# Seven blocks of z kept side by side in float32, with one cast and one subtraction a pair

## The reference

```python
h   = maximum(layernorm(x), 0)                  # x is (8192, 256)
mask = (adj > 0);  deg = sum(mask, axis=1)      # adj is (8192, 8192) int32
agg = mask @ h / maximum(deg, 1)
self_f = h @ W_self + b_self
nb_f   = agg @ W_nb + b_nb
out = x + relu(concat(self_f, nb_f) @ W_comb + b_comb)
```

## Time and profile before

| | us |
|---|---|
| median of 3 runs | 914.53 (914.16 to 917.45) |
| the profiled execution | 915.82 |
| its span, first to last instruction | 914.0 |
| TensorE matmul busy | 896.9 (98%) |
| VectorE busy | 799.1 (87%) |
| ScalarE busy | 377.5 (41%) |
| GpSimd busy | 91.0 (10%) |

### The profile page before, as it was taken

One profiled execution on the slowest core, in us unless ns is written; L12 is line 12 of the kernel. 1 busy time (PEld: TensorE's weight loads), 2 busy tenths in 40 slices (PEclk: granted clock), 3 DMA queues, 4 the chain that ended last, 5 costly groups with the idle time before them and its releaser, 6 DMA issues. The chain is left out here.

```text
span 914.0 us, 19105 instructions
## 1 busy us (share of the span) xinstructions
PE 896.9 (98%) x7720; PEld 760.1 (83%) x7720; DVE 799.1 (87%) x1512; ACT 377.5 (41%) x358; POOL 91.0 (10%) x132
## 2 busy tenths in 40 slices
PE   7999899899999999999999999999999999999997
PEld 5555478788888888888888888888888888888886
DVE  5999898898998988898889888888899998888884
ACT  3999854233333333332333333333333333333320
POOL 2888820000000000000000000000000000000000
PEclk9999999999999999999999999999999999999999
DMA  6467769999999999999999999999999999999950
GB/s 213 162 220 274 265 233 391 400 370 388 376 384 377 378 380 377 373 370 368 367 380 377 389 392 370 381 365 364 358 374 372 380 386 379 369 376 376 398 211 22
DMA packets 61367, 312.80 MB, mean 342 GB/s; under 512 B 6880, under 2 KB 8032, under 8 KB 28512
## 3 DMA queue, kind: packets, MB, share of 16 engines
q1 hardware_dynamic: 60736, 311.06, 87.7%
q10 hardware_dynamic: 544, 0.52, 0.2%
HBM read 294.78 MB, written 16.78 MB: 341 GB/s over the span
## 5 line engine op out<-in xcount | busy, mean ns | idle before, releaser
L625 PE MATMUL banks<-t,operands 128*128 128x257 f16 x7168 | 786.5, 272 | 2.6 <-DVE work L757 2.6
L625 PEld LDWEIGHTS banks<-t,operands 128*128 128x128 fp8e4 x7168 | 698.3, 97 | 90.7 <-issue 2.8
L468 ACT ACTIVATE mask<-stage,few 128x2048 fp8e4<-128x2048 int32 x128 | 252.7, 1999 | 415.5 <-DVE turned L720 318.9
L705 DVE TENSOR_SCALAR mask<-stage 128x2048 uint8<-128x2048 int32 x128 | 154.5, 1226 | 5.8 <-DMA stage<-in_adj_dram 5.8
L565 PE MATMUL banks<-t,xh 128*128 128x512 f16 x384 | 89.3, 383 | 4.2 <-DVE t L698 3.1
L757 DVE TENSOR_TENSOR work<-banks,work 128x512 f32<-128x512 f32 x32 | 22.1, 692 | 74.8 <-ACT work L518 74.8
L734 DVE TENSOR_TENSOR operands<-turned,operands 128x1024 uint32<-128x1024 uint32 x64 | 78.4, 1225 | 8.8 <-DVE turned L720 0.5
L714 DVE STREAM_TRANSPOSE operands<-mask 128x512 uint32<-128x512 uint32 x128 | 83.1, 687 | 0.2 <-DVE t L693 0.2
L720 DVE STREAM_TRANSPOSE turned<-mask 128x512 uint32<-128x512 uint32 x128 | 80.8, 669 | 0.0
L736 DVE TENSOR_TENSOR operands<-turned,operands 128x1024 uint32<-128x1024 uint32 x64 | 78.2, 1222 | 0.0
L565 PEld LDWEIGHTS banks<-t,xh 128*128 128x128 f16 x384 | 37.7, 98 | 44.0 <-issue 4.6
(11 more groups left out here) (62 smaller groups left out, 391.4 us busy)
## 6 DMA issues: line engine op xcount, KB each, us to landing
stage<-in_adj_dram SPq DMA_DIRECT2D x256, 1024.0 KB, 8.5
out_dram<-operands SPq DMA_DIRECT2D x32, 256.0 KB, 2.8
xh<-in_x_dram SPq DMA_DIRECT2D x32, 256.0 KB, 9.5
own<-out_dram SPq DMA_DIRECT2D x32, 256.0 KB, 10.5
out_dram<-xh SPq DMA_DIRECT2D x32, 256.0 KB, 6.0
t<-in_x_dram SPq DMA_DIRECT2D x30, 256.0 KB, 4.4
turned<-in_x_dram SPq DMA_DIRECT2D x2, 256.0 KB, 5.4
t<-in_L_gnn_W_nb_dram ACTq DMA_DIRECT2D x1, 256.0 KB, 4.0
```

The lines of the kernel that those rows point to most:

```text
L468: act.activation(mask[:, b, :].bitcast(FP8), stage[:, b, :], ACT.Sigmoid, bias=steep, scale=STEEP, saturate=False).then_inc(formed_s, 1)
L625: mm = pe.matmul(banks[:, n, 0:width], bytes_of[:, c, :, s], t16[:, KQ * h + SUB * c + s, SLOT[n], 0:width], start=(h == 0 and c == 0 and ...
L705: dve.tensor_scalar(mask[:, b, :], stage[:, b, :], 0.0, float(MINUS_ONE_BYTE), ALU.is_gt, ALU.mult).then_inc(formed_v, 1)
```

## The change

- `kept` holds all seven blocks of z and the own part of a pair (1408 columns). Two places lie in the second slot of `operands`, the third in `work`. The eviction writes the own part first and four z blocks behind it; GpSimd writes its three blocks behind these. One cast of 896 columns and one subtraction of 896 columns replace two each. The next eviction into a place waits for the whole subtraction.
- The columns of `w12` lie in another order, and the projection's right side is a pattern of two runs of 256 columns.
- Pairs 3, 7, 11, ... have both tiles normalized by ScalarE; GpSimd leaves these out.
- The start: 22 transposes of the identity instead of 16; the bias loads go ahead of the first weight loads on SP's queue; GpSimd instead of VectorE spreads the biases into `b_wide`; the negated weights are made in two halves; the product of the biases comes ahead of the first projection, projections 0 and 1 follow each other, and the turns come after them by `TURNS_AFTER`; VectorE makes the low halves of w and of h(1) ahead of the next statistics.
- The first adjacency blocks are loaded, formed and transposed in other iterations. Of step 2, `make_third` comes ahead of the loop over r.

```diff
-WARM = 16
+WARM = 22
-DIRECT = 4
-W_SUM, W_F1, W_OWN, W_F2, W_MINUS = 0, P, 2 * P, 4 * P, 5 * P
+W_OWN, W_SUM, W_F1, W_F2, W_MINUS = 0, 2 * P, 3 * P, 4 * P, 5 * P
-FORM_STEPS_S = {20: A12, 22: A21}
-FORM_STEPS_V = {23: A22, 25: A11}
-TURN_STEPS_V = {24: A22, 26: A11}
+FORM_STEPS_S = {20: A12, 23: A21}
+FORM_STEPS_V = {19: A22, 21: A11}
+TURN_STEPS_V = {20: A22, 22: A11}
-NEXT_STEPS_V = {27: A22, 28: A11}
+NEXT_STEPS_V = {25: A22, 28: A11}
-LOAD_STEPS = {12: A12, 14: A21, 16: A22, 18: A11}
-NEXT_LOADS = {21: (1, A12), 23: (1, A21), 24: (1, A22), 26: (1, A11), 28: (2, A22), 29: (2, A11)}
+LOAD_STEPS = {10: A22, 11: A11, 13: A12, 15: A21}
+NEXT_LOADS = {20: (1, A22), 22: (1, A11), 23: (1, A12), 25: (1, A21), 27: (2, A22), 29: (2, A11)}
+TURNS_AFTER = {1: (2, 3), 2: (4,), 3: (5,), 4: (6, 7)}
 def norms_s(j):
-    return (0,)
+    return (0, 1) if j >= 3 and j % 4 == 3 else (0,)
 def norms_g(j):
-    return () if j < 3 else (1,)
+    return () if j < 3 or j % 4 == 3 else (1,)
...
+        KEPT = 2 * D + 7 * P
+        slot_1 = operands[:, 1, :, :].rearrange("p o w -> p (o w)").bitcast(F32)
+        kept = [slot_1[:, 0:KEPT], slot_1[:, KEPT:2 * KEPT], work[:, :, :, :].rearrange("p n c m -> p (n c m)")[:, 0:KEPT]]
+        def kept_z(j):
+            return kept[j % RING][:, 2 * D:KEPT].rearrange("p (c m) -> p c m", c=7)
...
             def store_own(j):
                 sp.wait_ge(evicted, j + 1)
-                sp.dma_start(out[j, :, :].rearrange("p (t d) -> p t d", t=2), kept_blocks(j)[:, 2:6, :].rearrange("p (t f) m -> p t (f m)", t=2)
-                             ).then_inc(own_stored[j % RING], DONE)
+                sp.dma_start(out[j, :, :], kept[j % RING][:, 0:2 * D]).then_inc(own_stored[j % RING], DONE)
...
             load_x(0)
             load_x(1)
+            sp.dma_start(b_cols, b_cols_in[:, :]).then_inc(b_loaded, DONE)
+            sp.dma_start(bc_row, b_comb.rearrange("(a n) -> a n", a=1).partition_broadcast(P)).then_inc(b_loaded, DONE)
             sp.dma_start(ws_t, w_self_t.rearrange("(h p) n -> p h n", p=P)).then_inc(w_loaded[0], DONE)
...
+            pool.wait_ge(b_loaded, 2 * DONE)
+            for m in range(2 * HALVES):
+                pool.tensor_copy(b_wide[:, m, :], b_cols[:, m:m + 1].to_broadcast([P, P])).then_inc(wide_ready, 1)
             root_of(0)
+            pool.wait_ge(sum_high, 1)
+            pool.tensor_scalar(w12[:, 0, :, W_MINUS:W_WIDE], w12[:, 0, :, W_SUM:W_F1], -1.0, None, ALU.mult
+                               ).then_inc(sum_negated, 1)
             pool.wait_ge(sum_ready, 1)
-            pool.tensor_scalar(w12[:, :, :, W_MINUS:W_WIDE], w12[:, :, :, W_SUM:W_F1], -1.0, None, ALU.mult
+            pool.tensor_scalar(w12[:, 1, :, W_MINUS:W_WIDE], w12[:, 1, :, W_SUM:W_F1], -1.0, None, ALU.mult
                                ).then_inc(sum_negated, 1)
-            for b in range(1, 3):
-                root_of(b)
+            root_of(1)
...
+                if j == 0:
+                    root_of(2)
...
-                    act.wait_ge(t_low, 2 * (j - RING) + 1)
-                act.activation(kept[:, j % RING, :, :], pair_ps[j % RING][:, :, :], ACT.Copy, scale=Z_SCALE).then_inc(evicted, 1)
+                    act.wait_ge(t_low, j - RING + 1)
+                act.activation(kept[j % RING][:, 0:4 * D].rearrange("p (a t w) -> p t a w", a=2, t=2),
+                               pair_ps[j % RING][:, :, :].rearrange("p t (a w) -> p t a w", a=2), ACT.Copy, scale=Z_SCALE
+                               ).then_inc(evicted, 1)
 
             def high_of_t(j):
-                act.wait_ge(evicted, j + 1)
-                act.activation(direct_in_t(j, 0), direct(j), ACT.Copy).then_inc(t_high, 1)
                 act.wait_ge(combined, j + 1)
-                act.activation(t16[:, j, DIRECT:7, 0:P], combos[:, j % RING, 0:3, :], ACT.Copy).then_inc(t_high, 1)
+                act.activation(t16[:, j, :, 0:P], kept_z(j), ACT.Copy).then_inc(t_high, 1)
...
-            project(0)
             pe.wait_ge(wide_ready, 2 * HALVES)
...
-            turn(2)
-            for j in range(1, PAIRS):
-                if j + 2 < PAIRS:
-                    turn(j + 2)
+            for j in range(PAIRS):
                 project(j)
+                for n in TURNS_AFTER.get(j, (j + 3,) if j >= 5 else ()):
+                    if n < PAIRS:
+                        turn(n)
...
             def low_of_t(j):
-                dve.wait_ge(t_high, 2 * j + 1)
-                dve.tensor_tensor(direct_in_t(j, P), direct(j), direct_in_t(j, 0), ALU.subtract).then_inc(t_low, 1)
-                dve.wait_ge(t_high, 2 * j + 2)
-                dve.tensor_tensor(t16[:, j, DIRECT:7, P:D], combos[:, j % RING, 0:3, :], t16[:, j, DIRECT:7, 0:P],
-                                  ALU.subtract).then_inc(t_low, 1)
+                dve.wait_ge(t_high, j + 1)
+                dve.tensor_tensor(t16[:, j, :, P:D], kept_z(j), t16[:, j, :, 0:P], ALU.subtract).then_inc(t_low, 1)
...
             low_of_h(0)
+            w_low(0)
+            low_of_h(1)
             for p in range(2, 4):
                 stats_of(p)
-            w_low(0)
+            dve.wait_ge(c_product, 1)
+            dve.tensor_tensor(c_row[:, :], pair_ps[2][:, 0, 0:D], bc_row, ALU.add).then_inc(c_ready, 1)
             shifts(1)
...
             make_second(2)
+            make_third(2)
             for r in range(PAIRS):
                 i = 2 * r + 3
                 merge_a(r)
                 outer_sums(r)
-                if r == 0:
-                    make_third(2)
```

More of the change, by code:

```diff
@@ L149, in x_pair @@
             return flat_t[:, p * PLACE:p * PLACE + 4 * D].bitcast(F32)
-        kept = operands[:, 1, :, :].rearrange("p o w -> p (o w)").bitcast(F32)[:, 0:RING * 4 * D].rearrange(
-            "p (n t d) -> p n t d", n=RING, t=2)
-        def kept_blocks(j):
-            return kept[:, j % RING, :, :].rearrange("p t (c m) -> p (t c) m", c=4)
-        def direct(j):
-            return kept[:, j % RING, :, :].rearrange("p t (h b m) -> p (t h) b m", h=2, b=2)[:, 0:4:3, :, :]
-        def direct_in_t(j, first):
-            return t16[:, j, 0:DIRECT, first:first + P].rearrange("p (h b) m -> p h b m", h=2)
+        KEPT = 2 * D + 7 * P
[3 more added lines that the diff above has]
+            return kept[j % RING][:, 2 * D:KEPT].rearrange("p (c m) -> p c m", c=7)
         w_sum = own[:, 0, 0, :].rearrange("p (h m) -> p h m", h=HALVES)
         w_second = own[:, 0, 1, :].rearrange("p (h m) -> p h m", h=HALVES)
-        combos = work
         flat_work = work[:, :, :, :].rearrange("p n c m -> p (n c m)")
@@ L493, in _ @@
             w_high_half(0)
+            high_of_h(1)
             for t in norms_s(2):
@@ L497, in _ @@
             for j in range(PAIRS + 2):
-                if j + 1 < PAIRS:
+                if 1 <= j < PAIRS - 1:
                     high_of_h(j + 1)
@@ L556, in project @@
                     pe.wait_ge(sum_ready, 1)
-                    pe.wait_ge(sum_negated, 1)
+                    pe.wait_ge(sum_negated, 2)
                 if j >= RING:
@@ L564, in project @@
                     for at, (half, i, w) in enumerate(steps):
-                        mm = pe.matmul(pair_ps[j % RING][:, t, :], h_t[:, j % RING, i, t, half, :],
-                                       w12[:, w, half, t * W_OWN:t * W_OWN + 2 * D],
+                        mm = pe.matmul(pair_ps[j % RING][:, t, :].rearrange("p (a n) -> p a n", a=2), h_t[:, j % RING, i, t, half, :],
+                                       w12[:, w, half, :].rearrange("p (a n) -> p a n", a=3)[:, 0:2 + t:1 + t, :],
                                        start=(at == 0), stop=(at == len(steps) - 1))
@@ L615, in product @@
                 if i == 0 and n == M4:
-                    pe.wait_ge(t_low, 2 * KQ)
+                    pe.wait_ge(t_low, KQ)
                     pe.wait_ge(ones_set, 2 * len(ONES_OF))
@@ L852, in _ @@
                 norm(2, t)
-            dve.wait_ge(b_loaded, 2 * DONE)
-            for m in range(2 * HALVES):
-                dve.tensor_copy(b_wide[:, m, :], b_cols[:, m:m + 1].to_broadcast([P, P])).then_inc(wide_ready, 1)
             for p in range(4, 6):
@@ L890, in _ @@
             dve.wait_ge(combined, PAIRS)
-            dve.wait_ge(t_low, 2 * PAIRS)
+            dve.wait_ge(t_low, PAIRS)
             make_second(1)
```

20 lines of the change are left out of this document (6 added, 14 removed).

## The result

The changed kernel takes 919.15 us (median of 16 runs) beside 914.21 us for the kernel before (16 runs): a ratio of 1.0049 with an interval from 1.0036 to 1.0062. It is slower, by about 4.5 us, where 910.0 us was predicted: clear of no change, and on the line of 0.5% itself.

A forecast was written before the change was run, and what follows sets the result against it. TensorE was taken to bound the steady preamble, with the adjacency products untouched. Start 2.0 + late gaps 2.2 + hand-over 0.3 = 4.5 us gained: 910.0 us against the median of 914.53 us, range 906.5 to 914.5 us.

The forecast's parts named there:

- I estimate the biases landed at 6.3 us: Start, GpSimd's copies ahead of the first root: root at 7.5 us, 0.5 us late, bounds 0 and 1.2.
- Nothing: Steady pairs of the preamble: merged cast and subtraction, moved normalizations and new outer wait were to change the time by nothing.
- The cover I named: Steady pair: ScalarE needs about 2.8 of 3.03 us, and TensorE's turn comes about 2.6 us after VectorE's low half.
- the slow rival: Preamble bound by a ring of ScalarE and VectorE, 0.35 us more a pair over 28 pairs: 919.8 us, chance 0.09.
- The late gaps: TensorE's gaps late in the preamble: 2.5 us expected instead of 4.7, so 2.2 us gained, bounds 0.5 and 4.7.
- The end gap: Last preamble gap, 1.3 us ahead of 114.83 us: it goes, since VectorE's two late blocks are asked for four steps sooner.
- Turn 26: Late preamble, the four transposes of pair 26: expected some 2.2 us late, before about 1.2.
- The hand-over: From preamble to adjacency stage, with its stall of 2.6 us at 171.9 us: 0.3 us gained, bounds -0.5 and 2.6.
- The clock rival: Clock falls in the new 2.4 us gap ahead of projection 2, costing 1.7 us: 911.7 us, chance 0.18.
- The ring of ScalarE and VectorE: Preamble: their chain of halves, statistics, subtraction, eviction and cast exceeds 6.06 us for two pairs: 919.8 us, chance 0.09.
- the old gap: Start: TensorE stood from 12.75 to 15.84 us ahead of the first projection, waiting for VectorE's second low half of w.
- the cast's price: Steady pair on ScalarE: one cast of 896 columns near 0.93 us, 0.12 us cheaper than the two before.

The follow-up runs named there:

- e1: The changed kernel with GpSimd's first root ahead of the four bias copies: 915.57 us, ratio 1.0012 to the kernel before.
- e5: The changed kernel with the first root ahead of the bias copies and VectorE's subtraction in two: 913.86 us, ratio 0.9991 to the kernel before.
- e6: e1 with VectorE's shifts behind the subtraction, which stays whole: 913.39 us, ratio 0.9986 to the kernel before.
- e3: The changed kernel with normalizations divided as before, one tile of every pair on ScalarE, the other on GpSimd: 918.49 us, ratio 1.0031 to the kernel before.
- e12: e6 with VectorE's low half of h(2) and third shift ahead of the statistics of pairs 6 and 7, and GpSimd's later roots one iteration later: 912.66 us.
- e4: The changed kernel with the third phase of step 2 back inside the loop, after the first merge: 919.31 us, ratio 1.0036 to the kernel before.
- e11: e6 with the normalizations divided between ScalarE and GpSimd as before: 913.23 us, ratio 0.9987 to the kernel before.
- e8: e1 with the load of block A22 of step 2 in iteration 28, as before, instead of 27: 917.62 us, ratio 1.0028 to the kernel before.
- e7: e1 with each own store issued as two transfers of 1 KB a partition: 918.0 us, ratio 1.0039 to the kernel before.
- e10: e6 with forming, turning and loading of the first adjacency blocks in the iterations of the kernel before: 918.98 us, ratio 1.0056 to the kernel before.
- e2: The changed kernel with VectorE's subtraction of 896 columns split into 512 and 384: 916.77 us, ratio 1.0018 to the kernel before.

## Why the prediction was wrong, step by step

**The step that failed first: "I estimate the biases landed at 6.3 us".** They landed at 8.9 us, and the first root stood behind them. The prediction named this as what would make it wrong, and bounded it at 1.2 us; it was 2.86 us on the root. Taking it back gave 3.8 us at projection 2 and 3.0 us on the median (e1); what goes beyond the root I put down to the clock, which fell with the gap of 3.34 us that the late root left ahead of the first turn. No row of the prediction stands behind the 6.3 us. The trace of before held the better number: the same load took 6.7 us from issue to landing there, so an issue at 2.1 us lands at 8.8.

**"Nothing", for the steady pair "while that holds".** The cover I named (ScalarE's 2.8 of 3.03 us) did hold. What I did not follow was what runs on GpSimd while VectorE subtracts. In the changed kernel VectorE stood ready when the root ended, and its subtraction of 896 columns met the normalization behind the root within 0.12 us of its start; that normalization took 1.47 us for 0.56. In the kernel before VectorE came 0.21 us after, and its subtraction gave way instead. The term put at nothing measured 3.8 us of gaps. What put VectorE ahead of the root, and how much of that is the merging itself, was not parted. Parted (e5 against e1) or moved aside (e6 against e1) the subtraction gives back 1.7 and 2.2 us of the median.

The Trainium skill ("SBUF — State Buffer", SBUF: two separate sides) describes the ports that VectorE and GpSimd share as a lock held for a whole instruction. The rows agree with it: of the two that meet, one keeps its time and the other is stretched (0.56 and 1.31 us in e3, 1.47 and 1.08 us in the changed kernel). The prediction quoted it beside the slow rival and gave it no price.

**The late gaps, 2.5 us expected, 4.4 found.** The end gap went as expected. Turn 26 was put 2.2 us late and came 2.5 us late. The gaps ahead of turn 25 (1.06 us flagged) and turn 29 (0.47) were not expected: at turn 25 GpSimd had stood 2.35 us for an eviction of ScalarE, until 91.84 us, and its normalization came behind that. The term of 2.2 us measured 0.3.

**The hand-over, 0.3 us expected, 2.5 found**: the mechanism was right, the size was wrong, and it lies at the end of the bounds (-0.5 to 2.6). Where the x load comes about 6 us or more after the first product, the stall is 2.6 to 3.1 us:

| kernel | x load after the first product | stall |
|---|---|---|
| e12 | 3.7 | 0 |
| e1 | 4.0 | 0 |
| e6 | 3.9 | 0.41 |
| e4 (third phase back) | 3.8 | 0.70 |
| the changed kernel | 4.5 | 0.1 |
| e11 (normalizations as before) | 4.2 | 1.38 |
| e8 (load later) | 4.6 | 0.86 |
| before | 6.0 | 2.57 |
| e7 (store in halves) | 6.4 | 2.89 |
| e10 (steps as before) | 6.45 | 3.05 |

Below 5 us the stall is 0 to 1.4 us and does not follow the load in order; what decides there stays open. Both the store in one piece and the earlier steps are needed; either taken back restores the whole stall. The prediction had the earlier steps ending a gap of the preamble, and no term for them at the hand-over. Which of e10's tables does it, the loads or the forming, was not parted.

**The rivals.** The clock rival was right about a mechanism that I held for less likely: the gap at projection 2 was 2.8 us, and that projection took 4.05 to 4.45 us instead of 2.76 in five of the ten experiments' profiles that had such a gap (e2, e6, e8, e10, e11). That is part of why executions of one kernel spread: for the changed one, spans of 914.7 us at a mean granted clock of 1.000 and 919.6 us at 0.994.

The Trainium skill ("TensorE: Matmul & The Clock Gate", What's actually happening) lets the gate look on a beat of its own; a gap that costs in some profiles and not in others agrees with that.

The ring of ScalarE and VectorE, the rival that gave 919.8 us, came near the time by luck and had the cause wrong: projections stayed 3.02 us apart (29.70 to 32.72 us) wherever no root stood behind a subtraction, and VectorE still had 4.5 us of idle ahead of its low halves between 40 and 80 us.

**Confirmed**: the projection's strided right side costs nothing (379 ns a matmul over the whole preamble), the moved low half of w removes the old gap, the clock is up from 15.5 us on (though it had been down from 11.8 to 15.5 us), the cast's price, and with the root repaired projection 2 at 22.89 us for 23.2. The 2.9 us that this gives at projection 2 do not reach the first product: it comes at 121.25 us in e1, 120.02 before, because the steady gaps take them.

## What to carry to other kernels

When a wait is put ahead of work on a queue, price the transfer by its own time from issue to landing in the trace before, not by its size, and ask what the first item behind the wait feeds. When two instructions are merged, look at what the neighbouring engine runs beside them: here the merged instruction was shorter in sum and cost about 2 us, because it met another engine's short one that was on the path. A tenth of a microsecond in the order of starts decided which of the two was held up, so read both starts and not only that they overlap. Read a flagged releaser against that engine's own rows: here it named ScalarE, which had been done for 3.7 us.

## What the runs showed of the hardware

- A load of 128 KB (one row broadcast to 128 partitions) took 6.7 to 6.8 us from issue to landing at the start of the kernel, whether issued at 2.11 us or, before, at 4.30; loads of 256 KB beside it had a median of 7.0 us.
- GpSimd's normalization of 256 columns took 0.56 us alone, and 1.45 to 1.50 us when VectorE's subtraction of 896 columns (1.08 us) began between 0.06 us before it and 0.13 us after it. When the subtraction began 0.18 us after it, the normalization kept its 0.56 us and the subtraction took 1.31 to 1.33 us (e3, e11).
- GpSimd's root of eight columns took 1.65 us, and 2.44 us when it began beside such a subtraction.
- The last own stores land 2.4 us later against the first product when each goes in two transfers of 1 KB a partition (x load after 6.4 us instead of 4.0).
- TensorE gaps of 2.30, 2.58, 2.72, 2.80, 2.98, 3.05, 3.14, 3.15 and 3.34 us were each followed at least once by a stretch at a lower granted clock (0.57 in e2's window, 0.60 in the changed kernel's, 0.68 in e10's), which cost 1.3 to 1.8 us beside the gap. A gap of 2.31 us (at 101.03 us in the changed kernel), one of 2.80 us (e1) and one of 3.03 us (e4) were followed by projections of 2.75 and 2.76 us.
